# Two-layer graph network on one Trainium2 core: second-layer gathers by block of edges, places read through a register, own rows multiplied in place

## The reference

```python
h = relu(layernorm(x)); x = x + layer0(h, src, dst)      # attention with 4 heads of 64
h = relu(layernorm(x)); x = x + layer1(h, edge_weight1, W, b, src, dst)

def layer1(feat, eweight, W, b, src, dst):
    msg = feat[src] * eweight
    agg = segment_sum(msg, dst, n)
    deg = segment_sum(ones, dst, n)
    h_neigh = agg / maximum(deg, 1.0)[:, None]
    return concatenate([h_neigh, feat], -1) @ W.T + b
```

## Time and profile before

| | us |
|---|---|
| median of 3 runs | 1508.46 (1506.63 to 1508.52) |
| profiled execution, its own time | 1506.97 |
| profiled execution, span from first to last instruction | 1505.2 |
| mean granted TensorE clock over the span | 0.852 of full speed |

### The profile page before, as it was taken

The page is one execution under the profiler, slowest core; times in us unless marked ns, Lnnn a source line. Parts: engine busy times, 40 slices in busy tenths (PEclk is TensorE's granted clock), DMA queues, the critical chain, the costliest instruction groups (busy, mean ns, idle before and its releaser), DMA issues. The chain is left out here.

```text
span 1505.2 us, 18496 instructions
## 1 busy us (share of the span) xinstructions
PE 1129.3 (75%) x4168; PEld 727.0 (48%) x4168; DVE 1045.7 (69%) x2507; ACT 602.0 (40%) x2297; POOL 881.6 (59%) x907
## 2 busy tenths in 40 slices
PE   2989588888988988988982005777777777787677
PEld 1434466666766666666651003343434343444346
DVE  3444778989989988988877885555555555555554
ACT  1111178888778778778783630000000000000002
POOL 0000777767767767767621216777777777777770
PEclk9999889999999999999996556777777777767879
DMA  5111676666766666666650013333333333333332
GB/s 155 43 56 70 186 201 190 194 189 191 196 175 192 196 179 188 197 177 192 176 160 25 0 48 107 107 106 105 105 105 105 105 106 106 105 106 105 106 102 86
DMA packets 77775, 197.21 MB, mean 131 GB/s; under 512 B 16106, under 2 KB 31846, under 8 KB 77670
## 3 DMA queue, kind: packets, MB, share of 16 engines
q0 software_dynamic: 56320, 173.07, 40.3%
q1 hardware_dynamic: 19602, 22.32, 4.6%
q10 hardware_dynamic: 1748, 0.64, 0.2%
HBM read 182.94 MB, written 13.03 MB: 130 GB/s over the span
## 5 line engine op out<-in xcount | busy, mean ns | idle before, releaser
L590 POOL DMA_INDIRECT ring<-qv_tab,v_src x440 | 435.5, 990 | 326.4 <-POOLq L199 150.1
L500 POOL DMA_INDIRECT h_ring<-h_tab,v_src x440 | 422.2, 960 | 161.5 <-PE bank L1163 68.5
L1163 PE MATMUL bank<-h_ring,hot 128*128 128x256 f32 x880 | 375.1, 532 | 134.8 <-DMA h_ring<-h_tab,v_src 68.2
L647 ACT ACTIVATE ring<-ring 128x64 f32<-128x64 f32 x1760 | 437.5, 334 | 0.0
L1196 DVE TENSOR_TENSOR acc_odd<-acc_odd,bank 128x256 f32 x440 | 185.2, 421 | 222.5 <-PE bank L1163 218.2
L1163 PEld LDWEIGHTS bank<-h_ring,hot 128*128 128x128 f32 x880 | 178.4, 242 | 314.9 <-DMA h_ring<-h_tab,v_src 222.7
L686 PE MATMUL bank<-kx,hotT 128*128 x880 | 244.0, 403 | 69.2 <-ACT hotT L608 67.8
L695 PE MATMUL bank<-ring,hot 128*128 128x261 f32 x880 | 260.9, 399 | 5.1 <-ACT ring L647 4.3
L686 PEld LDWEIGHTS bank<-kx,hotT 128*128 128x128 f32 x880 | 165.9, 197 | 126.2 <-issue 105.2
L1126 ACT COPY ownT<-bank 128x256 f32<-128x256 f32 x25 | 9.3, 372 | 524.3 <-PE bank L1140 524.3
L861 DVE TENSOR_TENSOR acc<-acc,bank 128x261 f32 x440 | 184.9, 420 | 43.3 <-PE bank L695 30.7
(11 more groups left out here) (217 smaller groups left out, 834.2 us busy)
## 6 DMA issues: line engine op xcount, KB each, us to landing
ring<-qv_tab,v_src POOLq DMA_INDIRECT x440, 3.7
h_ring<-h_tab,v_src POOLq DMA_INDIRECT x440, 2.7
qv_tab<-qv_out SPq DMA_DIRECT2D x25, 256.0 KB, 2.0
h_tab<-xs SPq DMA_DIRECT2D x5, 640.0 KB, 3.4
out_dram<-kx SPq DMA_DIRECT2D x24, 128.0 KB
xs<-in_x_dram SPq DMA_DIRECT2D x4, 640.0 KB, 8.0
kx<-in_x_dram SPq DMA_DIRECT2D x4, 640.0 KB
xs<-in_x_dram SPq DMA_DIRECT2D x1, 512.0 KB
```

Source lines behind the costliest of these rows:

```text
L500: pool.indirect_dma_start(ring(u), None, table, bass.IndirectOffsetOnAxis(ap=v_src[:, r:r + 1], axis=0)).then_inc(got[u], 16)
L590: pool.indirect_dma_start(one_step(r, 0, 2 * D), None, qv_tab, bass.IndirectOffsetOnAxis(ap=v_src[:, r:r + 1], axis=0)).then_inc(got[r % R ...
L647: A.activation(part, part, ACT.Copy, scale=one_step(r, EX + h, EX + h + 1)).then_inc(scaled, 1)
L1163: T_.matmul(bank[u % 4][:, 0:D], hot[:, u, :], h_ring[:, u, :], start=True, stop=True).then_inc(sums_done, 1)
```

## The change

- Projections: three more small DVE instructions in `select` (tables `e_count`, `e_place` of one row), a new helper on PE (`turn_src`, four transposes of `e_src`, after the ninth tile), and a new one on DVE (`read_turned_src`, one copy, after the tenth).
- Second layer: POOL issues 416 gathers, one for each block of edges, by the indices `e_idx[:, e]`, into RH = 64 places. From gather 64 on it waits for `sums_done`. SP waits for each pair of gathers and adds 2 to `landed`. PE waits on `landed` against a register, and reads its place of `h_ring` through a register; for every 20 steps it loads 20 places and 20 counts.
- DVE builds up to 12 steps ahead into HR = 20 places, with one signal for each step.
- Own rows: PE turns them directly from `xs`, one node tile for every 17 steps; the bias becomes a third, one-row matmul for each tile. The copies into `own` (line 1122) and the bias instruction (line 1183) are gone.

```diff
@@ projections @@
+                def turn_src():
+                    pe.wait_ge(pick_read, 6)
+                    for c in range(EC):
+                        last = T_.transpose(bank[7][:, c * ER:(c + 1) * ER], e_src[:, c, :], ident[0:ER, 0:ER])
+                    last.then_inc(picked, 1)
...
                     f(V.tensor_tensor(r_row[:, :], iota_s[:, :], t_row[:, :], ALU.subtract))
+                    V.tensor_scalar(e_count[:, :], r_row[0:1, :], 1.0, None, ALU.add)
+                    f(V.tensor_copy(e_place[:, :], r_row[0:1, :]))
+                    V.tensor_scalar(e_place[:, :], e_place[:, :], RH - 1, None, ALU.bitwise_and)
...
+                def read_turned_src():
+                    dve.wait_ge(picked, 7)
+                    V.tensor_copy(e_idx[:, :], bank[7][:, 0:ET]).then_inc(pick_read, 1)
@@ second layer, POOL and SP @@
-                pool_part(pool)
+                for e in range(ET):
+                    if e >= RH:
+                        pool.wait_ge(sums_done, min(STEPS, e - RH + NT))
+                    pool.indirect_dma_start(h_ring[:, e % RH, :], None, h_tab,
+                                            bass.IndirectOffsetOnAxis(ap=e_idx[:, e:e + 1], axis=0)).then_inc(h_got[e % RH // 2], 16)
+                for e in range(0, ET, 2):
+                    sp.wait_ge(h_got[e % RH // 2], (e // RH + 1) * 32)
+                    sp.sem_inc(landed, 2)
@@ second layer, ACT @@
-                    A.copy(own[:, :], xs[:, T, :]).then_inc(own_read, 1)
@@ second layer, PE @@
+                    T_.matmul(bank[5][:, 0:D], ones[0:1, :], b1s[0:1, :], start=False, stop=True).then_inc(own_done, 1)
+                for r in range(STEPS):
+                    if r % LOADED == 0:
+                        _, places = nc.values_load_multi_w_load_instructions(e_place[0:1, bass.ds(r, LOADED)], engines=[pe.engine],
...
+                        _, counts = nc.values_load_multi_w_load_instructions(e_count[0:1, bass.ds(r, LOADED)], engines=[pe.engine],
...
+                    pe.wait_ge(hot_ready, r + 1)
+                    if r >= 4:
+                        pe.wait_ge(sums_added, r - 3)
+                    pe.wait_ge(landed, counts[r % LOADED])
+                    T_.matmul(bank[r % 4][:, 0:D], hot[:, r % HR, :], h_ring[:, bass.ds(places[r % LOADED], 1), :], start=True, stop=True).then_inc(sums_done, 1)
@@ second layer, DVE @@
-                f(V.tensor_tensor(kx[:, :, :], kx[:, :, :], b1s[:, :].unsqueeze(1).to_broadcast([P, NT, D]), ALU.add))
+                    while built < min(STEPS, 2 * r + Q, r + LEAD):
+                        build(built)
+                        built += 1
```

More of the change, by code:

```diff
@@ L486, in body @@
                         dot_skip(T)
[L487 to L502, removed]
+                pairs(body, [staircase, select, nothing, read_dst, read_src, read_wgt, read_starts, read_reach, read_rows, read_turned_src])
         def load_node_tiles(eng, i):
@@ L1107, in gnn_kernel @@
             sums_done, sums_added, hot_ready = sem("n_sums_done"), sem("n_sums_added"), sem("n_hot_ready")
-            got, pool_part = gather_rows("h", h_tab, lambda u: h_ring[:, u, :], lambda u: [(sums_done, U, u + 1)])
+            h_got = [sem(f"h_got{n}") for n in range(RH // 2)]
+            landed = sem("landed")
+            own_turned, own_copied, own_done, own_added = [sem("own_" + n) for n in "turned copied done added".split()]
             @block.gpsimd
             def _(pool):
-                pool_part(pool)
@@ L1114, in gnn_kernel @@
-            own_read, own_turned, own_copied, own_done, own_added = [sem("own_" + n) for n in "read turned copied done added".split()]
+                for e in range(ET):
[3 more added lines that the diff above has]
+                                            bass.IndirectOffsetOnAxis(ap=e_idx[:, e:e + 1], axis=0)).then_inc(h_got[e % RH // 2], 16)
+            @block.sync
@@ L1141, in turn_own, with multiply_own @@
                     last.then_inc(own_turned, 1)
[L1143 to L1145 removed]
+                def multiply_own(T):
+                    pe.wait_ge(own_copied, T + 1)
+                    if T >= 1:
+                        pe.wait_ge(own_added, T)
                     for c in range(2):
[L1147 to L1148 removed]
@@ L1149, in _ @@
[L1149 to L1163, removed]
+                        T_.matmul(bank[5][:, 0:D], ownT[:, c, :], w1T[:, 2 + c, :], start=(c == 0), stop=False)
@@ L1165, in _ @@
             @block.vector
             def _(dve):
[L1167 to L1178, removed]
@@ L1179, in _, with add_own @@
-                for u in range(Q):
-                    last = build(u, slice(u, u + 1))
-                last.then_inc(hot_ready, 1)
-                f(V.tensor_tensor(kx[:, :, :], kx[:, :, :], b1s[:, :].unsqueeze(1).to_broadcast([P, NT, D]), ALU.add))
[L1184 to L1196, removed]
-                    add_own(i, i + LEFT)
+                def add_own(T):
+                    dve.wait_ge(own_done, T + 1)
+                    V.tensor_tensor(kx[:, T, :], kx[:, T, :], bank[5][:, 0:D], ALU.add).then_inc(own_added, 1)
@@ new lines, in build @@
+                def build(r):
+                    if r >= HR:
+                        dve.wait_ge(sums_done, r - HR + 1)
+                    V.tensor_scalar(hot[:, r % HR, :], iota_f[:, 0:P], v_loc[:, r:r + 1], v_wgt[:, r:r + 1], ALU.is_equal, ALU.mult).then_inc(hot_ready, 1)
+                built = 0
+                tiles = load_node_tiles(dve, 0)
+                for r in range(STEPS):
+                    while built < min(STEPS, 2 * r + Q, r + LEAD):
+                        build(built)
+                        built += 1
+                    if r > 0 and r % U == 0:
+                        tiles = load_node_tiles(dve, r // U)
+                    dve.wait_ge(sums_done, r + 1)
+                    if r >= 1:
+                        dve.wait_ge(sums_added, r)
+                    a = acc_odd[:, bass.ds(tiles[r % U], 1), 0:D].rearrange("p o d -> p (o d)")
+                    V.tensor_tensor(a, a, bank[r % 4][:, 0:D], ALU.add).then_inc(sums_added, 1)
+                    if r % OWN_EVERY == 12 and r // OWN_EVERY < NT:
+                        add_own(r // OWN_EVERY)
```

50 lines of the change are left out of this document (30 added, 20 removed).

## The result

The changed kernel takes 1481.9 us (median of 4 runs, 1477.65 to 1484.49) where the kernel before takes 1507.55 (4 runs): ratio 0.983, 95% interval 0.980 to 0.986. That is 26 us less. The forecast was 32 less, 1475.5 us; its range (1469 to 1485) holds the time. The profiled execution of the changed kernel took 1484.49 us with a span of 1482.7, 22.5 less than the span before.

The account below looks back on a forecast made before the run. POOL's issuing of gathers was taken to bound the second layer. POOL -36.0, select +1.1, turning +2.4, end +0.35 sum to -32.1; from 1506.97 that gives 1474.9, adjusted to 1475.5 us for the median; range 1469 to 1485.

Parts of the forecast that it names:

- The bound and the 24 gathers: Second layer: POOL's issue sets the stage at 1.2505 us a gather; 24 fewer gathers save 30.0 us.
- building further ahead costs POOL nothing that I can see: Second layer: DVE's builds leave the median gather at 946 ns, so more building ahead adds nothing on POOL.
- The bias instruction: Start of second layer: a gather stands still until DVE's bias ends; removing the instruction saves 5.97 us (bounds 0 and 5.97).
- the long second gather stays: Rival, second layer: the bias did not hold the gather; 5.97 us come back, 1481.5 us; chance 0.08.
- Select: Projections, DVE: three added instructions between `r_row` and `sel` cost 1.1 us, all on the path (bounds 0.6 and 1.6).
- Turning the sources: Projections, PE: waiting for line 465 plus four transposes costs 2.4 us; bounds 2.0 and 4.5, with a possible lower clock.
- The end: End of second layer: SP's relay 0.15, two last steps +0.5, earlier own-rows add -0.3; sum +0.35 us.
- more than 6 us behind the last gather: Sign of being wrong: the stage after the second layer starts over 6 us behind the last gather.
- two register loads, 1.36 us each for 20 values: Second layer, PE: new loads for every 20 steps cost 2.3 us in 17 steps, at either clock.
- can PE keep up: Second layer: PE needs 16.9 of 20.1 us in 17 steps, slack 3.2 us, so its added work is hidden.
- The slower rival: Second layer: new waits and register reads make PE the bound; slower from 0.26 us a step, 1526 at 0.30; chance 0.05.
- with a PE that keeps up POOL never waits: Second layer: gather e waits only for step e - 39, so POOL's waits for PE cost nothing.

Follow-up runs that it names:

- eight profiles: Later and first profiles of kernels with the new tables as the change makes them; first layer's first gather at 158.4 us on the mean.
- the twelve later profiles: Profiles of the follow-up runs on two chips, original and edited kernels; there the kernel before took 1734.7 and 1731.1 us, the changed one 1760.0 and 1755.1.
- the short lead: Changed kernel with POOL allowed only 15 steps ahead instead of 39: 1725.2 us, ratio 0.996 to the kernel before.
- 4-byte counts: Changed kernel with the table of counts as 4-byte instead of 2-byte integers: 1739.6 us, ratio 1.005 to the kernel before.
- the first measurements: Changed kernel against the kernel before, four runs each, chip not recorded: 1481.9 against 1507.55 us, ratio 0.983.

## Why the prediction was right, and where it was off

*The bound and the 24 gathers.* Right in the measurement that it was made for: POOL's issue sets the stage, 1.25 us a gather, and no wait of POOL is longer than 0.30 us. The 519.0 us of the forecast were 520.1. The missing 1.1 us are intervals of up to 1.31 us that turn up now and then. The builds take 374 ns on the mean where they took 352, so the step "building further ahead costs POOL nothing that I can see" may have been a little off; that the two belong together isn't shown.

*The bias instruction.* Right, 5.97 us, and its cause is shown by putting it back. The rule of the Trainium skill ("SBUF — State Buffer", Who interferes with whom: a VectorE instruction with two inputs in SBUF contends with a GpSimd instruction that reads SBUF) agrees with the four profiles that have the instruction (one gather of 6.80 to 6.92 us each); the inference beside it, that descriptors are not held up, does not hold for an indirect DMA. The rival "the long second gather stays" is out.

*Select.* 1.1 forecast; the matrices come 1.02 us later (from `r_row` to `sel` 1.65 us instead of 0.63), and PE's tiles 0.94.

*Turning the sources.* 2.4 forecast, taken from one idle time of 1.7 us and four transposes: idle 1.71, transposes as forecast, 1.60 us on PE's tiles here and 1.9 on the mean of eight profiles. So both terms of the projections were sound and a little high, and what made 6.4 us of 3.5 is something else: 1.47 us that were lost before any added instruction and 2.37 us at the lower clock, ahead of `turn_src`. I had held such a spell possible (bound 4.5), as a consequence of `turn_src`, and not taken it.

*The end.* 0.35 forecast, 4.0 measured, and the step that failed is the path. I had counted the relay (0.25: SP passes on at 1440.91, PE's weight load follows at 1441.16) and two steps; they make DVE's last work end 1.2 us later than in the kernel before, counted from the last gather. But the output stage does not start then: DVE is idle for 3.34 us (1.34 before). By the trace's semaphore records the other four engines have signalled the end of the stage by 1443.9 us (1469.1 before), and POOL, which collects these signals, passes on at 1446.9 (1470.2), 8.6 us behind the end of its last gather (5.3 before). In the twelve later profiles, where POOL's last gather lies 13 us and more behind it, DVE's idle time is 0.32 us. So the stage ends when POOL is ready, 3.3 us later than before, and the relay and the two steps are hidden under that. Why POOL needs 8.6 us and not 5.3 stays open. The output stage itself took 0.8 us longer. My own sign of being wrong, "more than 6 us behind the last gather", was badly set: it is 9.8 us here, but it was 6.5 in the kernel before.

*The first layer.* Nothing forecast, 2.1 us measured from first to last gather. No edit touches it, and its cause stays open.

*The register loads.* Another step that failed, without harm to the number: "two register loads, 1.36 us each for 20 values". The row was of 4-byte elements, and the second table has 2-byte ones. With 4.73 us the loads take 5.2 us of 17 steps and not 2.3, and by the forecast's own sum PE's need is 19.8 of 20.1 us. PE's slack of 3.2 us, on which "can PE keep up" rested, would have been nearly nothing. Measured from 921 to 1437 us, PE is busy for 335.9 of 516 us at a mean granted clock of 0.79 (0.76 in the kernel before), which is 13.1 us in 17 steps; with the loads 18.3, a slack of 1.8 (it would be 15.4 with loads of 1.36 us, where the forecast had 16.9). Nor was it the 39 steps of room that kept the gain: no more than 7 were used. That the mistake cost nothing was luck, a slack that happened to be wide enough.

*The number.* 26 us measured for 32 forecast. In the two profiled executions 9.6 us are missing: 1.1 of the gathers and the bias, 3.7 at the end, 2.1 in the first layer, and 2.9 in the projections, which the tables' own cost does not explain. The four runs of the changed kernel themselves lie 6.8 us apart, and the profiled one is the slowest of them.

*The slower rival.* I gave it 0.05, with a cost of each step's waits as its price. Under late signals the kernel is slower, 1.2 to 1.5%, and PE does fall back in the second layer, but not by the new waits and register reads that I had named: the signals of PE come late in the kernel before as well. Two things of the change then cost: the long lead, which the step "with a PE that keeps up POOL never waits" counted as pure cover (30 us, by the short lead), and the load of 2-byte values (16 to 20 us of the second layer). The short lead together with 4-byte counts and two loads was not run.

## What to carry to other kernels

Room between a producer and a consumer is not free cover: where the consumer is the slower one, a longer lead only moved work behind the last transfer here, and cost 30 us. Ask what is left to do there if the lead is full. Cost a register load by its element size as well as by its count. Pair the n-th wait with the n-th signal before you call a signal late: the latest product is often not the one that is waited for. A version that keeps the fewer gathers and limits POOL's lead to 15 steps was the fastest where signals were late, by little (0.996, 0.992 to 0.999); whether it keeps the 0.983 of the first measurements was not measured. The trace of the changed kernel there speaks for it, since POOL never was more than 7 ahead.

## What was not expected of the hardware

- A register load of 20 values: 1.36 us from 4-byte elements, 4.73 us from 2-byte ones, shown by changing the type alone.
- Signals from PE, to DVE and to ACT, that queue up and come through in order, one in 5 to 6 us where it is worst, so that a product is taken up to 37 us after its end. They are in all twelve profiles of two chips: 71 to 92 late adds of 440 in a second layer, and none of a product that ended behind the last gather. In the first measurements there were none at all. Why they arise, and why the chips or times differ, stays open.
- The stage behind a run of indirect DMAs does not start before POOL is ready for it, 5.3 and 8.6 us behind the end of its last gather in the first measurements, though every other engine is done.
- The same program took 1507 us in one place and 1731 to 1735 us in others, by such signals; a change can be 1.7% faster in the one and 1.2% slower in the other.
